# A grouped convolution, a linear layer and routed low-rank experts: another opening, other places for the edge products, and the copy of the turned weighted rows on VectorE

## What is computed

```python
conv = conv1d(x, weight, groups=4, taps=9, pad=4) + (cond @ c_weight.T)[:, :, None] + bias
base = conv @ base_W.T + base_b
probs = softmax(conv @ router_W.T + router_b)        # 15 routes
topk_p, topk_i = top_k(probs, 8)
w = sum over the 8 chosen routes of topk_p, by expert_map[topk_i]   # 8 weights for each row
h = conv @ A.T                                       # 8 experts x 16
out = x + base + (h * w) @ B * 2.0
```

## Time and profile before

| | before |
|---|---|
| median of 3 runs | 184.37 us |
| the profiled execution's own time | 184.34 us |
| its span in the profile | 182.5 us |
| TensorE busy | 178.0 us, 98% |
| TensorE weight loads busy | 170.9 us, 94% |
| VectorE busy | 151.0 us, 83% |
| GpSimd busy | 139.7 us, 77% |
| ScalarE busy | 81.6 us, 45% |
| TensorE clock granted over the span | 0.999 |

### The profile page before, as it was taken

How to read it: one execution, slowest core, us unless ns; L and a number is a source line. 1 busy time by engine, 2 the same in 40 slices (tenths; PEclk the granted TensorE clock), 3 DMA queues, 4 the chain that set the end, 5 groups by cost and what they waited for, 6 DMA issues and landing times.

```text
span 182.5 us, 3929 instructions
## 1 busy us (share of the span) xinstructions
PE 178.0 (98%) x1236; PEld 170.9 (94%) x1236; DVE 151.0 (83%) x510; ACT 81.6 (45%) x247; POOL 139.7 (77%) x138
## 2 busy tenths in 40 slices
PE   7999999999999999999999999999999999999993
PEld 3777999999999999999999999999999999999992
DVE  0597888898898889888888988889898888978673
ACT  3568743354544434454433445444344545422320
POOL 2118999999888898888889888888988888885610
PEclk9999999999999999999999999999999999999999
DMA  6999951767475654637475454756536721233304
GB/s 160 355 347 288 340 190 11 234 193 213 161 231 176 187 169 123 198 131 230 132 232 164 133 166 163 230 178 196 188 101 160 278 83 61 94 115 115 119 0 172
DMA packets 17876, 32.01 MB, mean 175 GB/s; under 512 B 1984, under 2 KB 3136, under 8 KB 17856
## 3 DMA queue, kind: packets, MB, share of 16 engines
q1 hardware_dynamic: 17424, 31.40, 53.7%
q10 hardware_dynamic: 432, 0.36, 0.6%
HBM read 23.36 MB, written 8.39 MB: 174 GB/s over the span
## 4 chain that ended last, share of the span: by engine, by line
PE 92%; DMA 5%; DVE 1%; ACT 0%; SPq 0%; issue 0%; DVEq 0%
PE wide_ps L604 61%; PE wide_ps L646 12%; PE conv_banks L590 11%; DMA wide_sb<-wide_w 3%; PE edge_bank L590 3%; PE conv_banks L604 2%; PE odd_bank L633 2%; DMA x_in<-x_first 2%; PE conv_banks L563 1%; PE conv_banks L561 1%; DVE xr L979 1%; ACT wide_hi L356 0%; SPq L257 0%; PE conv_banks L646 0%; PE edge_bank L633 0%
## 5 line engine op out<-in xcount | busy, mean ns | idle before, releaser
L604 PE MATMUL wide_ps<-wide_hi,y_hi 128*128 128x400 f32 (+1 forms) x248 | 66.1, 326 | 0.3 <-ACT wide_hi L356 0.3
L604 PE MATMUL wide_ps<-wide_hi,y_lo 128*128 128x400 f32 (+1 forms) x248 | 62.6, 312 | 0.0
L604 PE MATMUL wide_ps<-wide_lo,y_hi 128*128 128x400 f32 (+1 forms) x248 | 62.4, 312 | 0.0
L484 POOL TENSOR_TENSOR terms_lo<-terms,terms_hi 128x512 fp32r<-128x512 f32 x28 | 36.3, 1297 | 18.2 <-ACT terms_hi L385 18.2
L604 PEld LDWEIGHTS wide_ps<-wide_hi,y_hi 128*128 128x128 f32 x248 | 44.0, 188 | 2.5 <-ACT wide_hi L356 0.6
L604 PEld LDWEIGHTS wide_ps<-wide_lo,y_hi 128*128 128x128 f32 x248 | 45.9, 188 | 0.0
L604 PEld LDWEIGHTS wide_ps<-wide_hi,y_lo 128*128 128x128 f32 x248 | 45.8, 188 | 0.0
L502 POOL TENSOR_TENSOR y_lo<-y,y_hi 128x512 fp32r<-128x512 f32 x31 | 40.3, 1298 | 5.0 <-ACT y_hi L400 5.0
L479 POOL TENSOR_TENSOR xr<-xr,base_b_sb 128x512 f32<-128x512 f32 x32 | 41.7, 1302 | 0.0
L407 ACT ACTIVATE hw_hi<-odd_bank 128x128 fp32r<-128x128 f32 x31 | 8.6, 278 | 54.3 <-PE odd_bank L633 54.3
L779 DVE TENSOR_TENSOR xr<-wide_ps,xr 128x512 f32<-128x512 f32 x30 | 20.7, 691 | 5.3 <-PE wide_ps L646 4.0
(11 more groups left out here) (90 smaller groups left out, 308.8 us busy)
## 6 DMA issues: line engine op xcount, KB each, us to landing
xr<-x_rows SPq DMA_DIRECT2D x32, 256.0 KB, 3.6
out<-xr SPq DMA_DIRECT2D x31, 256.0 KB, 3.3
terms<-x_units SPq DMA_DIRECT2D x28, 256.0 KB, 2.8
edges<-x_edges SPq DMA_DIRECT2D x14, 256.0 KB, 3.2
wide_sb<-wide_w SPq DMA_DIRECT2D x4, 328.0 KB, 5.0
x_in<-x_first SPq DMA_DIRECT2D x3, 264.0 KB, 5.3
weights_sb<-conv_w SPq DMA_DIRECT2D x2, 192.0 KB, 5.8
x_in<-x_first SPq DMA_DIRECT2D x2, 132.0 KB, 2.8
```

Of the source, the lines that this page charges most:

```text
L484: nc.gpsimd.tensor_tensor(terms_lo[i % 2][:, :, :, :], terms[i][:, :, :, :], terms_hi[i % 2][:, :, :, :].bitcast(F32), ALU.subtract)\
L604: mm = nc.tensor.matmul(sums_of(t, k)[:, b, 0:columns[1] - columns[0]], a[k % 2][:, r, :], w[:, r, columns[0]:columns[1]], start=r == 0 an ...
```

## The change

1. **Tiles 2 and 3** come as terms and one pair of edges instead of as whole x (`FIRST = 2` tiles are loaded whole, `START - FIRST = 2` as `first_terms`), with their differences made by GpSimd (tile 2, and the edges) and VectorE (tile 3). TensorE convolves them in full 32-bit with the summed weights, 256 columns a product: three products for tile 2, two for tile 3 (`conv_whole` for `conv_later`). The weights shrink from 14 to 12 blocks.
2. **Opening.** ScalarE instead of VectorE makes tile 0's y_hi, between its second and third `wide_high`; VectorE makes `wide_low(0)` ahead of tile 0's y_lo; TensorE makes the product with wide_lo(0) earlier; `turn_hw(0)` comes ahead of the convolution of tile 3; loads are issued in another order; base_b comes as 128 rows from DRAM instead of one row broadcast.
3. **Rows of tiles 0 to 3** get their bias after the sums (`bias_sums` on GpSimd) instead of before.
4. **Edge products** of tiles 4, 6 and 8 move from the end of steps 1, 3 and 5 to steps 2, 4 and 6, ahead of `up`. `condition` is cut in two: its first two instructions, and `reach` (the former third).
5. **VectorE's order** is new in all steps to 27, and in steps 7 to 27 (tiles 6 to 26) VectorE copies the turned weighted rows to hw_hi itself.
6. SyncE loads the rows of x ahead of storing, in each step.

The core of the diff:

```diff
+FIRST = 2
+POST = 4
+        def dve_makes_hw_hi(t):
+            return from_tile(t, 6) and up_to_tile(t, TILES - 6)
...
             sync.wait_ge(x_loaded[1], 16)
             load_conv(2)
-            load_x(2)
-            sync.wait_ge(wide_in[0], 16)
-            load_conv(3)
-            load_x(3)
+            load_first_terms(0)
+            sync.wait_ge(wide_in[1], 16)
+            sync.dma_start(first_edges[:, :, :, :], x_edges[0]).then_inc(first_edges_in, 16)
+            load_conv(4)
             sync.wait_ge(wide_in[2], 16)
             load_terms(START, 0)
+            sync.dma_start(up_sb[:, :], up_w).then_inc(up_in, 16)
+            sync.wait_ge(wide_in[3], 16)
+            load_conv(3)
+            load_first_terms(1)
             load_edges(START // 2, 0)
-            sync.dma_start(up_sb[:, :], up_w).then_inc(up_in, 16)
-            sync.dma_start(base_b_sb[:, :], base_b.partition_broadcast(P)).then_inc(base_b_in, 16)
-            sync.dma_start(xr[0][:, :], x_rows[0]).then_inc(xr_loaded[0], 16)
             load_terms(START + 1, 1)
-            sync.wait_ge(x_loaded[3], 16)
+            sync.dma_start(xr[0][:, :], x_rows[0]).then_inc(xr_loaded[0], 16)
+            sync.dma_start(base_b_sb[:, :], base_b).then_inc(base_b_in, 16)
+            sync.wait_ge(first_terms_in[1], 16)
...
-            wide_high(range(RUNS))
+            wide_high(range(2))
+            act.wait_ge(y_ready, 1)
+            nc.scalar.activation(y_hi[0][:, :, :], y[0][:, :, :], ACT.Copy).then_inc(y_hi_first, 1)
+            wide_high(range(2, RUNS))
...
-                hw_high(t - 1, k - 1)
+                if not dve_makes_hw_hi(t - 1):
+                    hw_high(t - 1, k - 1)
...
+            pool.wait_ge(wide_lo_ready, RUNS)
+            pool.wait_ge(first_terms_in[0], 16)
+            nc.gpsimd.tensor_tensor(first_terms[0][:, 0], first_terms[0][:, 0], first_terms[0][:, 1], ALU.subtract)
+            pool.wait_ge(first_edges_in, 16)
+            nc.gpsimd.tensor_tensor(first_edges[:, 0], first_edges[:, 0], first_edges[:, 1], ALU.subtract)
             conv_low(1)
             y_low(1, 1, 2)
             edge(START // 2, 0)
...
                 if t == 0:
+                    up_low()
                     terms_low(t + 4, k)
-                    up_low()
                     edge_low(p + 2, k // 2)
...
                 linear(1, 1, runs, (FRONT_BANK,), (Y_REST,)).then_inc(front_done, 1)
-                conv_later(3)
                 turn_hw(0, 0)
                 linear(1, 1, runs[:3], (NEXT_BANK,))
                 up(0, 0)
                 linear(1, 1, runs[3:], (NEXT_BANK,)).then_inc(linear_done, 1)
+                conv_whole(3)
+                conv_blocks(START, 0)
...
                     linear(t, k, runs[:2], (NEXT_BANK,))
+                    if t in (2, 4, 6):
+                        conv_edges(t + 2, (k + 2) % GROUPS, p + 1).then_inc(conv_done, 1)
                     up(t - 1, k - 1)
...
             def hw_low(t, k):
+                if dve_makes_hw_hi(t):
+                    dve.wait_ge(hwt_done, t + 1)
+                    nc.vector.tensor_copy(hw_hi[k % 2][:, :], hwt_of(t)).then_inc(hw_hi_ready, 1)
                 dve.wait_ge(hw_hi_ready, t + 1)
```

More of the change, by code:

```diff
@@ L544, in step @@
                         edge(p + 3, 1 - k // 2)
+                if from_tile(t, 3) and up_to_tile(t, POST + 1):
+                    bias_sums(t - 2)
             steps_of(step)
@@ L584, in conv @@
                 if t < 2 * START and h == 0:
                     pe.wait_ge(conv_lo_ready, 2 + g // 2 * 2)
-                for n, (sums, j, hi, lo) in enumerate(parts):
-                    if n == 2:
-                        pe.wait_ge(edge_lo_ready, p - START // 2 + 1)
-                    for w, a in ((conv_hi, hi), (conv_lo, hi), (conv_hi, lo)):
-                        mm = nc.tensor.matmul(sums, w[:, j, :], a[:, :, :],
-                                              start=w is conv_hi and a is hi, stop=a is lo)
+                products(conv_ps[:, h, 0, :, :], S_SUM[g], terms_hi[h][:, 1], terms_lo[h][:, 1])
@@ L641, in up @@
                     for a, w in ((hw_hi, up_hi), (hw_hi, up_lo), (hw_lo, up_hi)):
+                        if w is up_lo and not from_tile(t, 1):
+                            pe.wait_ge(up_lo_ready, 1)
                         if a is hw_lo and n == 0:
@@ L1048 @@
         "up_w": np.asarray(L0_ffn_B).transpose(0, 2, 1).reshape(E * R, L),
[L1049 removed]
+        "base_b": np.tile(np.asarray(L0_ffn_base_b), (P, 1)),
     }
```

266 lines of the change are left out of this document (179 added, 87 removed).

## The result

The changed kernel takes 186.39 us (median of 7 runs, 186.22 to 186.74), the kernel before 184.75 on the same chip (184.21 to 185.95): ratio 1.0096, 95% interval 1.0071 to 1.0121. It is outside the range, on the slow side. The profiled execution took 186.39 with a span of 184.6, against 184.34 and 182.5.

A forecast was written before the change was run, and what follows sets the result against it. TensorE, busy 98% of the span, was taken as the bound. The terms -0.37 - 0.86 + 0.10 + 0 + 0.3 + 0.3 + 0 = -0.53 us, against 184.34, gave 183.8 us, range 183.1 to 185.0.

The forecast's parts named there:

- Part 1: Convolution of tiles 2 and 3: less matmul on TensorE; 0.37 us saved for tile 2, 0.86 for tile 3.
- 1.13: Opening's net gain in us: 0.37 and 0.86 from the convolutions of tiles 2 and 3, less 0.1 lost.
- Part 2: First step: ScalarE's later y_hi mostly hidden; GpSimd's two differences delay tile 1's y_lo, 0.1 us lost.
- 0.1 later than before in effect: Opening: the third high product starts about 10.8 with one product more behind it, so y_hi's delay hardly counts.
- 10.36: Opening: when TensorE's wait for a late wide_hi part ends; from there the chain was taken as TensorE alone.
- Part 3: `up(0)`: edges must land by 15.9 for up_lo; they were taken to land at 15.7, so 0 lost.
- rival C: Edges land late, up_lo is late, TensorE waits 0.3 to 1.0 us in `up(0)`: 184.1 to 184.8, chance 0.17.
- Part 4: Steps 5 to 7: two hand-overs from VectorE to TensorE get longer, 0.3 us lost at each.
- the two hand-overs: Weighted rows of tile 5 to be turned, and hw_hi of tile 6: each reaches TensorE 0.3 us late.
- Part 5: Steps 7 to 27: VectorE's copy takes 0.28 us, its step 4.89 against TensorE's 5.13; 0 lost.
- Rival D: VectorE becomes the bound in steps 7 to 27: 184.5 to 186.5 us, likeliest 185.1, chance 0.16.
- the reading under which the prediction let the new order save nothing: VectorE's next op starts only once the pipe is empty, so only the copy would count; the forecast's sum kept overlap.

The follow-up runs named there:

- e2_yhi_dve: The changed kernel with VectorE instead of ScalarE casting the high part of tile 0's activations, right behind its turning: 187.05 us, ratio 1.012.
- e1_act_copy: The changed kernel with ScalarE instead of VectorE making the copy to hw_hi in all steps: 185.1 us, ratio 1.0026.
- e9_copy_from_10: The changed kernel with VectorE making the copy from step 10 on instead of from step 7: 186.01 us, ratio 1.0087.
- e3_shallow: The changed kernel with the order of steps 2 to 4 kept up to step 28 and ScalarE copying throughout: 186.13 us, ratio 1.0079.
- e14: As e1_act_copy, but VectorE draws level spread over steps 6 to 9: 185.61 us, ratio 1.0053.
- e13: As e1_act_copy, but the order of steps 2 to 4 holds up to step 20 and VectorE draws level from there: 185.73 us, ratio 1.0068.
- e11: As e6, with ScalarE casting tile 0 one weight piece earlier and, in step 29, making hw_hi ahead of tile 30's activations: 185.84 us, ratio 1.0085.
- e6: As e3_shallow, but VectorE draws level gradually in steps 26 to 29 instead of all at once in step 28: 186.08 us, ratio 1.0089.
- e15_order_copy: The kernel before with the changed VectorE order from step 2 and VectorE's copy in steps 7 to 27, old opening: 184.89 us, ratio 1.0011.
- e4_copy_alone: The kernel before with VectorE making the copy in steps 7 to 27, its order otherwise unchanged: 192.49 us, ratio 1.042.

## Why the prediction was wrong

**Part 1: the cut is right.** Five pieces of 0.43 replace four of 0.86. In the best profiles of the new opening (31.8 from the first rows to `turn_hw(4)`, against a middle of 33.1 with the old one) all of the 1.3 us arrives, more than the 1.13 forecast.

**Part 2: the failed step is "0.1 later than before in effect" for ScalarE's y_hi.** It took the cast's end from a profile in which the weight pieces had landed early (9.05; it was 9.37), and it took 10.36, where TensorE had waited for the third piece, as a floor that covers it. In the changed kernel nothing covers it: in all eight profiles with the cast in this place `turn_hw(0)` starts 8.08 to 8.12 behind the start of the cast. Whether the cast is late depends on a load. In five of the eight it costs nothing that shows; in the changed kernel's profile it costs 0.55 (10.13 against 9.58), and the front of tile 1 began at 14.81 in the chain instead of 14.38. Moving the cast does not help by itself: in e2_yhi_dve GpSimd's two differences end within tenths of the same time.

**Part 3: 0 forecast, 0.27 in the profile** (step 1 lasts 6.32 instead of 6.05). The landing was mis-sized:
```profile
edges<-x_edges SPq DMA_DIRECT2D x1, 256.0 KB, 5.3
```
The edges were issued at 10.85 and landed at 16.15, where the rate had given 16.1 and 15.9 was the limit; the prediction took 15.7 instead, "without its drag". But the drag of the broadcast lay behind the edges: before, they landed at 14.57, the next transfer at 15.66 and base_b at 17.53. So rival C's wait came (POOL's up_lo in `up(0)`, its sign), just below its 0.3 to 1.0, and "the edges land in time" was wrong in this kernel. It holds in three of the eight profiles of this opening.

**The opening together.** In the changed kernel's profile 1.30 less 0.55 and 0.27 leaves about 0.5 against the middle of the old openings. The kernel before's own profile had lost 0.28 of its own (33.37 against 33.09), and the changed kernel's first rows came 0.33 later, by the landing of the first loads; with these the 0.46 of the table comes out. The middle of the eight profiles is 32.1, a gain of 1.0: over many executions 1.13 would not have been far off.

**Part 4: the places right, the sum 0.6 for 1.44.** hw of tile 5 came 0.3 late, as worked out. Missing were the low part of hw of tile 4, which stands behind `turn(6)` in step 5 (`up(4)` 0.95 instead of 0.71), and most of the copy's first step: 0.3 was taken from a sum in which every instruction starts as early as it can, and e1_act_copy and e9_copy_from_10 show 0.5 for the copy, on top of 0.2 that step 7 loses without it. The deeper error is that the two hand-overs were costed one by one. In steps 2 to 4 VectorE is one tile less ahead: it turns tile t+1 in step t where it must come to turn tile t+2. Counted up to the low part of hw in a step, that is a turning and a condition, 0.7 + 0.9 = 1.6 us of work on an engine with 0.15 of slack in a step. e3_shallow shows that without drawing level steps 5 to 7 lose 0.2. Drawing level costs 0.95 in steps 5 to 7 (e1_act_copy, those 0.2 included), 1.3 in steps 7 to 9 (e14), 1.4 in steps 21 to 23 (e13), and 1.5 to 1.8 at the end (e11, e6, e3). That slack does not add up, since the next thing VectorE could do (the low part of hw) waits for TensorE, is the reading that fits all of these; it is argued, not tested by itself.

**Part 5: right for the steps by themselves, wrong here.** Copy 0.29, overlaps 0.08, no wait of TensorE in a usual step; e15_order_copy bears the row sum out: order and copy together cost no more than 0.2 from 7 to 27 (106.41 against 106.20) in the old opening. Rival D's mechanism, VectorE as the bound, did not come; that its 184.5 to 186.5 holds the measured time is luck. The failed step is the **0** for steps 8 to 27, where 1.06 came. Of this the copy costs 0.84 (107.26 against 106.42): 0.4 in the gap at step 20, which reaches TensorE because the copy lies on its path, and 0.02 to 0.03 per step. The other 0.22 stand without the copy too (106.42 against 106.20), and 0.14 of them with the new order in the old opening (106.34). The creep lies over single matmuls with no wait listed and stays open; e15_order_copy has hardly any of it.

**Sum by the terms as measured in the profiles:** -0.46 (opening) + 1.44 (steps 5 to 7) + 1.06 (to step 27) + 0.08 (tail) = 2.12, for a difference in span of 2.1 and of the medians of 1.6 to 2.1. No version with the new opening beat the kernel before; the best, ScalarE's copy (e1_act_copy), stands at +0.26%. The bias after the sums (change 3) and the loads ahead of stores (change 6) were not taken back by themselves; e1_act_copy has both, so together with the rest they cost no more than its 0.5 us and what its opening gained.

## What to carry to other kernels

A shorter opening that leaves a nearly full engine a tile less ahead is a loan: cost the drawing level as the whole of that work, at one place, before counting the gain (here 1.6 us of work cost 0.95 to 1.8). An operation moved onto such an engine is nearly free only with the order that hides its latency and only from the step where that engine is level (7.9 us, 1.3 us and about 0 for the same copy). Compare openings from the first landed data, not from time zero, and over several profiles: this one varied by 1.4 us, in the two places that wait for a load.

## What the runs showed of the hardware

**The same add overlaps on one half of the partitions and not on the other.** In the rows of steps 14 and 15 above, reach is the same instruction on partitions 64 to 127 (90.21) and on 0 to 63 (95.25), behind a MAX8 that starts on partition 0. The latter starts 0.09 before MAX8 ends (95.16 + 0.18), the former 0.03 after it (90.00 + 0.18). It is so in all 21 steps of this order in the profile, 0.08 before or 0.03 behind in turn. The Trainium skill (VectorE: DVE Perf Modes, "Two Vector instructions with no wait between them") says that an instruction starts only when all earlier ones have finished if its inputs or its output start in another group of 32 partitions than the last ones did; for this pair the trace agrees.

**Overlap of independent instructions.** They start 0.07 to 0.09 before the end of the one ahead, so the reading under which the prediction let the new order save nothing fails here. The Trainium skill (VectorE: DVE Perf Modes, "The DRAIN you can't avoid") itself adds, in the paragraph that the prediction drew on, that a next op which is not held starts earlier; the trace agrees. The 7.6 us between e4_copy_alone and e15_order_copy are no measure of this overlap alone, since the order also moves the waits between engines.

**Late starts at fixed places of VectorE's list.** At its 64th, 192nd, 320th, 448th and 576th record an instruction can start up to 0.4 us late, in 14 of the 17 profiles at one of them at least. With three records fewer ahead of it (e9_copy_from_10) the same copy starts on time.

**A broadcast row loads slower.** In the five profiles of the old opening base_b, one row of DRAM broadcast to 128, landed 1.2 to 1.9 us behind the transfer ahead of it; as 128 full rows of the same 256 KB it landed 0.7 behind in the changed kernel's profile.

**The landing of the first loads** varies by 1.3 us between profiles with the same issues (first rows from 6.22 to 7.55), and moves the rest with it.
